# A graph network of three attention layers: a sixth score bank in layer 1, pairs in layer 0, four countings of edges at four steps, shorter staging rings

## The reference

```python
# layer 0: scores from Wh @ a1 (rows) and We @ a2 (columns)
e = leaky_relu(u[:, None] + v[None, :], 0.2)
e = where(adj > 0, e, -9e15)
h = elu(softmax(e, axis=1) @ entity_embs + x)
x = layernorm(x + h)
# layers 1 and 2, on the same mask
for i in range(2):
    Wh = h @ W[i]
    e = leaky_relu(u + v.T + c, 0.2)
    att = softmax(where(mask, e, -9e15), axis=1)
    h = 0.2 * x + 0.8 * elu(att @ Wh)
    outs.append(h)
out = layernorm(x + concat(outs) @ mlp_w + mlp_b)
```

## Time and profile before

| | |
|---|---|
| median of 3 runs | 3445.28 us (3441.72 to 3446.64) |
| the profiled execution's time | 3447.01 us |
| its span | 3445.2 us |
| TensorE busy | 3096.8 us (90%) |
| VectorE busy | 2865.5 us (83%) |
| ScalarE busy | 2274.0 us (66%) |
| GpSimd busy | 280.9 us (8%) |
| moved by DMA | 679.29 MB |

### The profile page before, as it was taken

One profiled execution on the slowest core, in us unless ns is written; L12 is line 12 of the kernel. 1 busy time (PEld: TensorE's weight loads), 2 busy tenths in 40 slices (PEclk: granted clock), 3 DMA queues, 4 the chain that ended last, 5 costly groups with the idle time before them and its releaser, 6 DMA issues. The chain is left out here.

```text
span 3445.2 us, 56585 instructions
## 1 busy us (share of the span) xinstructions
PE 3096.8 (90%) x21977; PEld 1071.2 (31%) x21977; DVE 2865.5 (83%) x5292; ACT 2274.0 (66%) x3934; POOL 280.9 (8%) x330
## 2 busy tenths in 40 slices
PE   1479999999999999699999999997999999999998
PEld 0123333333333333233333333332333333333333
DVE  5468888888888876699999999997888788888886
ACT  0247776666766767477777777784666666666665
POOL 0000000000000000000000000001112112211211
PEclk9989999999999999899999999998999999999999
DMA  8999999999999981221312222214667766766764
GB/s 242 287 346 342 342 338 338 335 341 333 342 341 332 342 259 55 86 86 64 112 71 105 79 96 87 88 62 135 166 158 166 188 155 161 178 167 163 170 150 80
DMA packets 441759, 679.29 MB, mean 197 GB/s; under 512 B 297474, under 2 KB 318082, under 8 KB 416914
## 3 DMA queue, kind: packets, MB, share of 16 engines
q1 hardware_dynamic: 409458, 564.40, 51.2%
q0 software_dynamic: 32032, 111.27, 16.2%
HBM read 430.10 MB, written 77.69 MB: 147 GB/s over the span
## 5 line engine op out<-in xcount | busy, mean ns | idle before, releaser
L1235 DVE SCALAR_TENSOR_TENSOR eps<-ua,v8col,cb 128x512 f32<-128x512 f32 x2800 | 1963.9, 753 | 294.5 <-ACT prob L630 218.4
L630 ACT ACTIVATE prob<-eps,v2col 128x512 f32<-128x512 f32 x2392 | 1526.2, 689 | 599.1 <-PE eps L810 588.9
L851 PE MATMUL acc<-prob,feat 128*64 128x512 f32 x4784 | 1216.5, 605 | 6.4 <-ACT acc_s L638 6.4
L810 PE MATMUL eps<-nt,nbig 128*64 128x512 fp8e4 (+2 forms) x6642 | 997.5, 385 | 150.7 <-DVE eps L1235 146.5
L810 PEld LDWEIGHTS eps<-nt,nbig 128*64 128x64 bf16 (+2 forms) x6642 | 327.7, 103 | 1032.0 <-DVE eps L1235 687.7
L851 PEld LDWEIGHTS acc<-prob,feat 128*64 128x64 f32 x4784 | 305.9, 137 | 381.7 <-issue 208.0
L1065 DVE TENSOR_SCALAR mi<-stage 128x1024 uint8<-128x1024 int32 x512 | 351.7, 688 | 66.4 <-DMA stage<-in_adj_dram 66.0
L630 ACT ACTIVATE mi<-eps,v2col 128x512 f32<-128x512 f32 x344 | 219.5, 687 | 102.0 <-PE eps L810 100.3
L630 ACT ACTIVATE stage<-eps,v2col 128x512 f32<-128x512 f32 x336 | 214.6, 687 | 95.1 <-PE eps L810 93.4
L860 PE MATMUL den<-prob,ones 128*32 128x512 f32 x2048 | 275.5, 610 | 0.0
L1074 DVE TENSOR_SCALAR edges<-nt 128x2048 int32<-128x2048 int32 x192 | 234.0, 1219 | 29.7 <-PE misc L821 15.2
(11 more groups left out here) (175 smaller groups left out, 1810.4 us busy)
## 6 DMA issues: line engine op xcount, KB each, us to landing
stage<-in_adj_dram SPq DMA_DIRECT2D x512, 512.0 KB, 6.8
nt<-nt_d SPq DMA_DIRECT2D x128, 1024.0 KB, 6.1
nt_d<-nt SPq DMA_DIRECT2D x64, 1024.0 KB, 7.1
prob<-prob POOLq DMA_DIRECT2D x64, 512.0 KB, 5.8
mi<-mi POOLq DMA_DIRECT2D x64, 512.0 KB, 6.4
stage<-stage POOLq DMA_DIRECT2D x64, 512.0 KB, 6.6
ub<-u_d SPq DMA_DIRECT2D x48, 256.0 KB, 5.2
xy_d<-xin POOLq DMA_DIRECT2D x32, 256.0 KB, 3.3
```

The costliest lines, as they stand in the source:

```text
L630: nc.scalar.activation(weights(l, b, j), eps[:, j % ES, :], ACT.Exp, bias=v2col[:, j:j + 1]).then_inc(s_p, 1)
L810: mm = nc.tensor.matmul(et[c:c + cols, :], nbig[:, c:c + cols], edge, start=False, stop=True, skip_group_check=True, tile_position=(0, c))
L851: mm = nc.tensor.matmul(acc[h:h + C, :], feat[:, l % 2, j, 0:C], weights(l, b, j), start=(k == 0), stop=(k == NT // 2 - 1))
L1235: dv.scalar_tensor_tensor(eps[:, j % ES, :], ua[:, par, :], v8col[:, j:j + 1], cb[:, par, :], ALU.add, ALU.max).then_inc(s_fill, 1)
```

## The change

- Layer 1 may use `den`, idle there, as a sixth bank of scores: `BANKS = (5, 6, 5)`, and `bank` says which one a tile has. The first use waits for the last copy of layer 0's denominators.
- Layer 0 sums by pairs two pairs back as the other layers do; its denominators come once in eight tiles (`two_quads`, at steps 3, 11, 19, ...). Its masks are 64 columns wide (`HALF`).
- `prob` has 12 slots. To make room, the staging ring has 4 buffers (`SS`) and the mask ring 6 (`MR`). In layer 2 the 24 slots are 12 of `prob`, 4 of `mi`, 8 of `stage`.
- The four parts of edges are counted at steps 33, 36, 40, 43, and the last two made at 39 and 42, for 40 and 41.

```diff
-MR = 8
+MR = 6
-SS = 5
+SS = 4
-GROUP = (QUAD, 2, 2)
-LAG = (1, 2, 2)
+PAIRLAG = 2
-TS = 2 * QUAD
-SLOTS = (TS, TS, 3 * TS)
+LAST_RING = 6
+TS = 3 * QUAD
 ES = 5
+BANKS = (ES, ES + 1, ES)
-MASK_COLS = (32, 64, 64)
+HALF = 64
-T_XOR = (29, 32, 40, 41)
-T_HIST = (35, 35, 43, 43)
+T_XOR = (29, 32, 39, 42)
+T_HIST = (33, 36, 40, 43)
...
+        def bank(l, j):
+
+            n = j % BANKS[l]
+            return den[:, :] if n == ES else eps[:, n, :]
 
         def freed(l, b, j):
 
-            if j >= ES:
-                return tile(l, b, j) - ES + 1
-            last = max(i for i in range(NT) if i % ES == j)
+            if j >= BANKS[l]:
+                return tile(l, b, j) - BANKS[l] + 1
+            k = l if b else l - 1
+            last = max(i for i in range(NT) if i % BANKS[k] == j % BANKS[k])
             return tile(l, b, last) - NT + 1
...
             def probs(l, b, j):
 
-                if l < 2 and j % GROUP[l] == 0 and not (l == 0 and b == 0 and j < TS):
-                    act.wait_ge(s_main, summed(l, b, j - TS + GROUP[l] - 1))
...
+                if l < 2 and tile(l, b, j) >= TS and j % 2 == 0:
+
+                    old, i = divmod(tile(l, b, j) - TS, NT)
+                    ol, ob = divmod(old, NB)
+                    if ol == 1:
+                        act.wait_ge(s_main, pairs(ol, ob, i // 2 + 1))
+                    else:
+                        act.wait_ge(s_den, dens(ol, ob, i // DEN + 1))
...
-            def sums(l, b, k):
-
-                if l:
-                    main(l, b, k).then_inc(s_main, 1)
-                else:
-                    main(l, b, 2 * k)
-                    main(l, b, 2 * k + 1).then_inc(s_pair, 1)
-                    denominators(l, b, k).then_inc(s_main, 1)
+            def two_quads(l, b, g):
+                denominators(l, b, 2 * g)
+                denominators(l, b, 2 * g + 1).then_inc(s_den, 1)
...
                         mask_scores(l, b, t, par, mask_cols(l, t, head, tail))
-                        if t % GROUP[l] == GROUP[l] - 1:
-                            k = t // GROUP[l] - LAG[l]
+                        if t % 2 == 1:
+                            k = t // 2 - PAIRLAG
                             if k >= 0:
-                                sums(l, b, k)
+                                main(l, b, k).then_inc(s_main, 1)
...
+                        if l == 0 and t % DEN == DLAG:
+                            g = t // DEN - 1
+                            if g >= 0:
+                                two_quads(l, b, g)
+                            elif tail:
+                                two_quads(l, b - 1, NT // DEN + g)
...
                 if not (l == 0 and b == 0 and j < ES):
                     dve.wait_ge(s_p, freed(l, b, j))
+                    if (l, b, j) == (1, 0, ES):
+                        dve.wait_ge(s_dene, NB)
                 elif j == 0:
                     dve.wait_ge(s_prime, 1)
-                dv.scalar_tensor_tensor(eps[:, j % ES, :], ua[:, par, :], v8col[:, j:j + 1], cb[:, par, :],
+                dv.scalar_tensor_tensor(bank(l, j), ua[:, par, :], v8col[:, j:j + 1], cb[:, par, :],
                                         ALU.add, ALU.max).then_inc(s_fill, 1)
```

More of the change, by code:

```diff
@@ L260, in build @@
         s_p = sem("probs_done")
-        s_pair = sem("pair_of_probs_summed")
         s_main = sem("probs_used")
@@ L318, in places @@
         def places(b, j):
-            q, o = divmod((b * NT + j) % SLOTS[2], TS)
-            return (prob[:, :, :], more, rest)[q], o
+            n = (b * NT + j) // QUAD % LAST_RING
+            buf = (prob[:, :, :], prob[:, :, :], prob[:, :, :], as_probs(mi[:, 0:QUAD, :]),
+                   as_probs(stage[:, :, :]), as_probs(stage[:, :, :]))[n]
+            return buf, (0, QUAD, 2 * QUAD, 0, 0, QUAD)[n] + j % QUAD
         def weights(l, b, j):
             if l < 2:
-                return prob[:, j % SLOTS[l], :]
+                return prob[:, tile(l, b, j) % TS, :]
             buf, o = places(b, j)
@@ L347, in den_blocks, with pairs, dens @@
             return b if l == 0 else (l - 1) * NB + b
[L349 to L357, removed]
+        def pairs(l, b, n):
+            return (l * NB + b) * (NT // 2) + n
+        def dens(l, b, n):
+            return den_blocks(l, b) * (NT // DEN) + n
         def started(l, b, j, on_act):
@@ L567, in add_probs @@
                 for h in range(2):
-                    pool.wait_ge(s_main, group(2, b, 4 * g + 2 * h + 1) + 1)
+                    pool.wait_ge(s_main, pairs(2, b, 4 * g + 2 * h + 2))
                     buf, o = places(b, DEN * g + QUAD * h)
@@ L615, in start_scores @@
                     act.wait_ge(s_ub[par], ub_count(l, b, par))
-                nc.scalar.activation(eps[:, j % ES, :], ub[:, par, :], ACT.Relu, bias=v8col[:, j:j + 1],
+                nc.scalar.activation(bank(l, j), ub[:, par, :], ACT.Relu, bias=v8col[:, j:j + 1],
                                      scale=1.0 - ALPHA).then_inc(s_filla, 1)
             def probs(l, b, j):
-                if l < 2 and j % GROUP[l] == 0 and not (l == 0 and b == 0 and j < TS):
-                    act.wait_ge(s_main, summed(l, b, j - TS + GROUP[l] - 1))
@@ L623, in probs @@
                 if l == 2 and j % DEN == 0:
[L624 to L628, removed]
+                    ahead = LAST_RING * QUAD
+                    if b == 0 and j == 0:
+                        act.wait_ge(s_main, pairs(2, 0, 0))
+                    elif b or j >= ahead:
+                        c, i = divmod(b * NT + j - ahead, NT)
+                        act.wait_ge(s_den, den_done(c, i // DEN))
@@ L629, in probs @@
+                if l < 2 and tile(l, b, j) >= TS and j % 2 == 0:
[5 more added lines that the diff above has]
+                        act.wait_ge(s_den, dens(ol, ob, i // DEN + 1))
                 act.wait_ge(s_z, tile(l, b, j) + 1)
-                nc.scalar.activation(weights(l, b, j), eps[:, j % ES, :], ACT.Exp,
+                nc.scalar.activation(weights(l, b, j), bank(l, j), ACT.Exp,
@@ L631, in probs @@
                                      bias=v2col[:, j:j + 1]).then_inc(s_p, 1)
             def sums_out(l, b, par):
-                if l:
-                    act.wait_ge(s_main, group(l, b, NT // GROUP[l]))
-                else:
-                    act.wait_ge(s_pair, (b + 1) * (NT // QUAD))
+                act.wait_ge(s_main, pairs(l, b, NT // 2))
                 nc.scalar.activation(acc_s[:, :], acc[:, :], ACT.Copy).then_inc(s_acce, 1)
             def denominators_out(l, b):
[L641 to L644, removed]
+                act.wait_ge(s_den, dens(l, b, NT // DEN))
@@ L785, in mask_cols @@
             def mask_cols(l, j, head, tail):
-                n = GROUP[l]
-                first = j // n * n - 1
+                first = j // 2 * 2 - 1
                 whole = []
@@ L795, in mask_cols @@
                     whole += [T_FOLD, T_HEADT, T_ROWS]
-                return P if any(first <= t < first + n for t in whole) else MASK_COLS[l]
+                return P if any(first <= t < first + 2 for t in whole) else HALF
             def mask_scores(l, b, j, par, cols):
                 on_act = j in ON_ACT[l]
-                et = eps[:, j % ES, :]
+                et = bank(l, j)
                 m, o = divmod(j, MT)
@@ L1013, in _ @@
                 blocks(body)
[L1014 to L1019, removed]
+                for k in range(NT // 2 - PAIRLAG, NT // 2):
+                    main(l, NB - 1, k).then_inc(s_main, 1)
+                if l == 0:
+                    two_quads(l, NB - 1, NT // DEN - 1)
+                for g in DEN_ORDER if l == 2 else ():
+                    if DEN * (g + 1) + (ADDLAG if g in ADDED else DLAG) >= NT:
+                        eight_probs(NB - 1, g)
                 for t in range(NT):
```

11 lines of the change are left out of this document (4 added, 7 removed).

## The result

| | before | changed |
|---|---|---|
| median | 3444.1 us | 3409.35 us (3406.14 to 3415.37) |
| ratio | | 0.990, interval 0.9886 to 0.9914 |
| span of the profiled execution | 3445.2 us | 3405.8 us |
| first mark (layer 0's first block summed) | 250.75 | 244.31 |
| layer 0, first mark to last | 1139.3 | 1117.2 |

The change makes the kernel 1.0% faster, 35 us, which is small but clear of the noise; the forecast was 3403. A mark is ScalarE's copy of `acc`, one a block, as in the earlier trace rows; a layer's time here goes from its first mark to its sixteenth. Between layers lies what neither kernel does differently: 101.9 us before and 102.2 after the change behind layer 0, 102.2 and 103.0 behind layer 1.

What follows compares the result with a forecast made beforehand. TensorE bounds layer 0; TensorE and VectorE are level in layer 1. Layer 0 -20, start +5, layer 1 -27, layer 2 0: -42 from 3447.0 gives 3405.0, less 1.7 for the median: 3403 us, range 3362 to 3440.

Steps and rivals of the forecast that it cites:

- the signs named for being wrong: Layer 0's marks scatter or stand at 76.8 us, or layer 1's stay over 56.4 us.
- C: Rival, chance 0.08: layer 1 gains nothing, as TensorE, 0.4 us fuller, is what VectorE waits for; 3436 us.
- The sixth bank: Layer 1: VectorE starts one score tile more before waiting; -1.9 us, layer 1 in all -1.8 us a block.
- the bound (TensorE gets the same wait elsewhere): Layer 1: end of the range at which the block gains 0 us; the other end was -2.85.
- Layer 0: Layer 0's blocks: -2.5 + 0.2 - 0.4 + 0.6 + 0.7 = -1.4 us, taken 14 times: -20 us.
- The width of the masks: Layer 0, TensorE: fewer changes of matmul width with 64-wide masks and denominators of eight tiles; -2.5 us a block.
- The four places: Countings at four places add changes of width on TensorE: +0.6 us a block in layer 0, +0.4 in layers 1 and 2.
- layer 0 is TensorE's: Layer 0: TensorE sets the block's time, since block 14, with few masks and transfers, was only 1.75 us shorter.
- The ring of four: Layer 0's adjacency loads: four staging buffers make one mask a block 0.7 us late; +0.7 us a block.
- A: Rival, chance 0.12 with its half: the ring of four sets layer 0's pace, blocks 82.0 us; 3506 us, half 3469.
- The start: Some 50 starved units at the start lose 0.1 us each with four staging buffers: +5 us, bounds 0 and +26.
- Layer 2: TensorE's wait at step 47 takes up the added 0.4 us: 0, bounds -0.4 and +0.9 us a block.

Runs made afterwards that it cites:

- Late_five: Changed kernel with five banks in layer 1 instead of six and the head's steps two later (53, 58, 59): 3414.1 us.
- head_late: Changed kernel with the head's steps two later (T_HEAD 53, T_HEADT 58, T_ROWS 59): 3395.9 us.
- old_counts: Changed kernel with the countings back at steps 35, 35, 43, 43 and the edges at 29, 32, 40, 41: 3418.3 us.
- quads: Changed kernel with layer 0 doing the sums of four tiles in one piece after four masks, as before the change: 3434.2 us.
- wide32: Changed kernel with layer 0's masks 32 columns wide again, as before the change: 3435.3 us.
- five_banks: Changed kernel with five banks of scores in layer 1 again instead of six: 3419.2 us.
- ring5: Changed kernel with five staging buffers, four mask buffers and each mask waiting for the transpose of four pairs ago: 3402.6 us.

## Why the prediction was right, and where it was not

The time was 3409 for 3403 and the sign was right, but the sum came out by parts that were off both ways. Against the profiled executions the forecast was 42 us and 39 were measured: layer 1 gave 20 us less than forecast, and the start (11 us better), layer 2 (5) and layer 0 (2) made up for it. That the total came so close is luck. Of the signs named for being wrong, two showed: layer 0's marks scatter, and layer 1's stand at 56.45, over the 56.4 given for C.

- **The sixth bank** is the step that failed. It gave 0.27 us a block, with the counting places 0.41, where I had 1.8 (-27 us for layer 1, measured -7). I read VectorE's and TensorE's waits as one queue too short. It is a queue, but VectorE's step 51 needs TensorE's step 47, and from step 21 to 47 TensorE did not wait once: being ahead of it there buys only an earlier wait for the counts. VectorE's waits for a bank in layer 1 were to fall under 0.7 us a block; they fell to 1.2, and 0.8 for the counts came in. Late_five against head_late shows the same bank worth 1.18 us when that cap is off, and the last block of layer 1, which has no counts to wait for, 0.69. The forecast named the bound (TensorE gets the same wait elsewhere) as the end of a range and rival C as its case, with 0.08, but C's reason, a fuller TensorE, is not what was found: old_counts takes the changes of width away and is slower; the row that spoke for it was in the earlier trace rows, VectorE's 1.5 us for the turned counts in layer 0.
- **Layer 0** came out in size (-22 us, forecast -20), by other terms. The width of the masks gave 1.4 us a block where I had 2.5 for both widths; its price in TensorE's time was right, but most of it stays hidden while VectorE makes masks as well (1.0 us a block up to block 13, 2.9 in block 14). The even feed of pairs, which I had at nothing, gave 1.3 us (quads: layer 0 18 us longer over its marks, the first mark 6 us later). The four places gave some 0.4, not far from the scatter, where I charged 0.6. These are worths of one edit taken out at a time. They make 3.1 us a block, less 0.4 to 1.4 for the ring, against 1.6 measured, so they need not add up. Denominators of eight tiles and the 12 slots of `prob` were not tried alone. So "layer 0 is TensorE's" was half the truth: block 14's 75.05 us showed that VectorE and transfers had slack, not that TensorE had none.
- **The ring of four** cost 19 us in the kernel before and 7 in the changed one; I had 0.7 x 14 + 5 = 15. As forecast the lateness is mostly covered, and the average (9.6 us for a slot against 7.5) held, so A's pace never set in. But it is not one mask a block that is late: the block shown has five waits, 5.0 us in all, and over the run the waits grew by 72 us where I had 5 to 35.
- **The start**: first mark 6.4 us sooner where I had +5. It is 249 to 251 us in wide32, quads and the kernel before (with either ring), 244 to 248 in the rest, so it goes with pairs and widths, not with the ring; five_banks at 248.1 shows the scatter, so this is seen and not shown.
- **Layer 2**: forecast 0, measured -5; 4.6 of it are one block of 70.09 us of the kernel before, whose transfers landed late.
- What the profile was to show: layer 0's marks in place, but with the scatter that I had put down as a sign of A. It was A's mechanism at a tenth to a fifth of its price (7 to 19 us of 88).

## What to carry to other kernels

Before you lengthen a queue, look for the step at which the leading engine needs a result of the one behind: the distance of the two steps caps the lead, and a longer queue is worth little beyond it (here 0.27 us a block under the cap, 1.18 without it). When a wait goes and its time does not, read which new row stands in the table of waits; here one row of 0.8 us pointed at a number (47) whose change by one gave 38.5 us on top of the edit's 35, half of it in a layer for which it was not meant. A total that is right can be made of wrong terms: compare by stretch, not by the end.

## What the runs showed of the hardware

- A change of the matmul's column width costs 0.09 to 0.15 us in the stream: 0.10 to 0.11 from masks into the f32 sums (718.24 in the earlier trace rows, wide32), 0.15 from the sums to the next width (the same places), 0.09 and 0.12 around a counting.
- Landing times of a load hardly fell with fewer in flight: 6.8 us in the median with a ring of five, 6.5 with four in the kernel before; 6.9 (ring5) and 6.6 in the changed one.
- Marks of layer 0 repeat to 0.01 us in the kernel before, where from block 3 to 13 VectorE waits for no transfer, and scatter by up to 2.7 us in the changed one. But a wait for a transfer does not by itself break the repetition: in head_late blocks of 74.88 us hold waits of 0.4 to 5.7 us. What repeats tells that the waits for transfers are covered, not that there are none.
